# Scores ahead of attention, smaller pieces of weight work among VectorE's steps, and products of ones on TensorE in a fused attention and expert kernel

## The reference, cut to what matters

```python
# attention, ctx the 64 context rows of a sequence
kp = ctx @ Wk.T; vp = ctx @ Wv.T + bv; qp = layernorm(x) @ Wq.T + bq
x = x + softmax(qp @ kp.T / sqrt(128)) @ vp @ Wo.T + bo
# experts, E = 8, K = 2, F = 512
t = layernorm(x)
probs, idx = top_k(softmax(t @ Wr + br), 2); probs = probs / probs.sum()
h = layernorm(relu(t @ W1[e] + b1[e])) * g1[e] + be1[e]
y = layernorm(relu(h @ W2[e] + b2[e])) * g2[e] + be2[e]
x = x + sum over the 2 experts of probs * y
```

## Time and profile before

| | us |
|---|---|
| timed runs, median (lowest to highest) | 297.57 (297.2 to 300.11) |
| profiled execution | 300.53 |
| its span, first to last instruction | 298.8 |
| TensorE busy | 247.1 |
| VectorE busy | 246.1 |
| ScalarE busy | 215.3 |
| GpSimd busy | 192.2 |

### The profile page before, as it was taken

How to read it: one execution, slowest core, us unless ns; L and a number is a source line. 1 busy time by engine, 2 the same in 40 slices (tenths; PEclk the granted TensorE clock), 3 DMA queues, 4 the chain that set the end, 5 groups by cost and what they waited for, 6 DMA issues and landing times.

```text
span 298.8 us, 9992 instructions
## 1 busy us (share of the span) xinstructions
PE 247.1 (83%) x2765; PEld 193.0 (65%) x2768; DVE 246.1 (82%) x1109; ACT 215.3 (72%) x799; POOL 192.2 (64%) x302
## 2 busy tenths in 40 slices
PE   2788558898799767976987999999999797999980
PEld 2354346555466534456876988999999786999520
DVE  0758947765678698987998989999999797999996
ACT  1355536674945768864989998999999797999820
POOL 8802275746463655777676876788887675878550
PEclk9999655557855775699999999999999999999995
DMA  6996294121311332345222323233334656452338
GB/s 171 340 289 206 63 313 154 55 64 54 125 53 53 91 107 71 88 95 127 57 65 53 77 62 74 57 76 75 75 73 66 185 146 134 130 145 65 98 114 281
DMA packets 48801, 34.56 MB, mean 116 GB/s; under 512 B 26934, under 2 KB 42870, under 8 KB 48747
## 3 DMA queue, kind: packets, MB, share of 16 engines
q1 hardware_dynamic: 39100, 22.83, 27.7%
q0 software_dynamic: 6592, 9.00, 10.7%
q10 hardware_dynamic: 3056, 2.11, 2.4%
HBM read 15.14 MB, written 12.02 MB: 91 GB/s over the span
## 4 chain that ended last, share of the span: by engine, by line
PE 31%; POOL 22%; issue 16%; DVE 11%; DMA 7%; SPq 6%; ACT 5%; POOLq 2%; DVEq 0%; ACTq 0%
PE bank L726 13%; PE bank L730 13%; POOL answers L684 10%; POOL words_of L710 7%; POOL slot_rows L672 4%; SPq L520 4%; PE bank L791 2%; DMA x_tok<-in_x 2%; DMA kb_room<-slot_rows 2%; SPq L553 1%; DVE w2f L1620 1%; DMA answers<-vo,words_of 1%; PE bank L776 1%; DMA w_mean<-w_sums 1%; ACT w1l L1193 1%
## 5 line engine op out<-in xcount | busy, mean ns | idle before, releaser
L672 POOL DMA_INDIRECT slot_rows<-pay,pos x64 | 65.8, 1027 | 44.8 <-DVE pos L1575 27.4
L684 POOL DMA_INDIRECT answers<-vo,words_of x71 | 69.8, 984 | 32.4 <-ACT vo L1363 21.2
L726 PE MATMUL bank<-kb_room,w1h 128*128 128x128 f16 x568 | 55.0, 219 | 9.2 <-DMA kb_room<-slot_rows 3.8
L730 PE MATMUL bank<-w2h,rh 128*128 x284 | 51.4, 219 | 2.2 <-ACT w2l L1099 1.6
L726 PEld LDWEIGHTS bank<-kb_room,w1h 128*128 x568 | 42.2, 97 | 15.9 <-issue 10.4
L730 PE MATMUL bank<-rh 128*128 128x129 f16 x284 | 51.5, 220 | 0.0
L730 PE MATMUL bank<-w2l,rh 128*128 x284 | 51.4, 219 | 0.0
L726 PE MATMUL bank<-kb_room,w1l 128*128 128x128 f16 x284 | 51.1, 219 | 0.0
L1321 ACT ACTIVATE rh<-bank 128x512 f16<-128x512 f32 x71 | 41.9, 590 | 11.3 <-PE bank L726 9.5
L1839 DVE SCALAR_TENSOR_TENSOR xk<-bank,rh 128x512 f16<-128x512 f32 x71 | 47.9, 674 | 0.0
L710 POOL DMA_DIRECT2D words_of<-slot_rows x71 | 40.7, 575 | 4.9 <-issue 4.6
(11 more groups left out here) (260 smaller groups left out, 612.3 us busy)
## 6 DMA issues: line engine op xcount, KB each, us to landing
x_tok<-in_x SPq DMA_DIRECT2D x8, 256.0 KB, 6.8
w1f<-in_L_ffn_W SPq DMA_DIRECT2D x2, 1024.0 KB, 9.3
pay<-pay SPq DMA_DIRECT2D x8, 256.0 KB, 2.7
w1f<-answers SPq DMA_DIRECT2D x8, 256.0 KB
w2f<-answers SPq DMA_DIRECT2D x8, 256.0 KB, 3.3
kb_room<-slot_rows SPq DMA_TRANSPOSE x71
words_of<-slot_rows POOLq DMA_DIRECT2D x71, 1.0 KB
answers<-vo,words_of POOLq DMA_INDIRECT x71
```

The costliest lines, as they stand in the source:

```text
L672: eng.indirect_dma_start(slot_words, bass.IndirectOffsetOnAxis(ap=pos[:, g % 2, k, i:i + 1], axis=0), pay[g % 2][:, k, i, :].bitcast(U32), ...
L684: eng.indirect_dma_start(answers, bass.IndirectOffsetOnAxis(ap=words_of[:, j % NW, 0:1], axis=0), z[j % NZ], None).then_inc(s_ans[j % NZ], 16)
L726: return eng.matmul(dst, lhsT, rhs, start=start, stop=stop)
L730: return eng.matmul(dst, lhsT, rhs, start=start, stop=False, skip_group_check=True)
```

## The change

- The scores of a group become one bias product of 256 columns and four products of 64 columns into bank 1, with keys in a tile of their own (`kq`). The 136 columns of x and its logits become a product of their own (`skip`) into banks 3 and 4. From step 2 on, two of the next group's four scores stand ahead of `attend`, two behind it; `skip` comes at the step's end. The maxima are one reduction over 256 columns instead of two over 128, and stand ahead of the statistics.
- `base_next` moves to the head of a step, `totals` with it in step 5.
- `keep(n)` is new: n bf16 products of ones, 128 by 128, into columns of bank 2 that nothing reads: 12 ahead of the first ranks, 10 ahead of the probabilities' transpose in steps 1 to 7, and 10 ahead of the ranks in steps 3 to 8.
- VectorE's tables name 22 places in a step and single pieces: `CENTRE` numbers the 32 pieces of W2. Its pieces now stand in steps 5 to 7. `weight_scale` is taken apart among the root steps of step 5; the gate's steps are taken apart around `picked` and `pos_`.
- SP makes the payload's copy ahead of the transfers of W2's sums, and the second of these in step 5 of its loop instead of 6; ScalarE's `w_rows_copy(0)` moves behind `x2_copy` in step 4.
- The tiles that lay in parts of `xk` (`part_rows`, `parts`, `shares` and others) get room of their own, and GpSimd's copy of identities into `xk` goes.

```diff
@@ -444,10 +440,16 @@
-        NONE = ((),) * 4
...
-        CENTRE = {4: ((), (), (), (0,)), 5: ((), (1,), (2,), (3,)), 6: ((), (), (4,), (5,)), 7: ((6,), (), (7,), ())}
...
+        LESS_LAST = {2: {2: (0,), 16: (1,), 17: (2,), 21: (3,)}, 3: {3: (4,), 5: (5,), 7: (6,), 9: (7,)}}
...
+        UP_LO = {7: {14: (3,)}, 8: {4: (4,), 6: (5,), 8: (6,), 10: (7,)}}
...
@@ -729,6 +727,13 @@
                 return eng.matmul(dst, lhsT, rhs, start=start, stop=False, skip_group_check=True)
+            ones_b = ones[:, :].bitcast(BF16)[:, 0:P]
+            def keep(n):
+                for _ in range(n):
+                    mm(bank[2][:, 3 * P:], ones_b, ones_b)
             done = []
             def ctxT(h):
...
@@ -776,25 +781,32 @@
                     t = eng.transpose(bank[0][:, i * P:(i + 1) * P], x[:, g * GT + i, :], ident[:, :])
                 t.then_inc(p_xT, 1)
-            def scores(g, b):
+            def score_bias(g):
                 n, first = (0, 0) if g * GT < FIRST else (1, FIRST)
-                if 2 * g + b >= 3:
-                    eng.wait_ge(s_x2, 2 * g + b - 2)
-                if g in (0, FIRST // GT) and b == 0:
+                if g >= 1:
+                    eng.wait_ge(s_prob, g)
+                if g in (0, FIRST // GT):
                     eng.wait_ge(s_sel, n + 1)
                     from_act(eng, f"sdT{n}")
-                    eng.wait_ge(s_ones, 4)
-                tiles = range(2 * b, 2 * b + 2)
-                at = g * GT + 2 * b - first
-                eng.matmul(pair(g, b)[:, :, 0:KEYS], sdT[n][:, :], kb_tile[n][:, at:at + 2, :], start=True, stop=False,
-                           skip_group_check=True)
+                mm(bank[1][:, 0:GT * KEYS], sdT[n][:, :],
+                   kb_tile[n][:, g * GT - first:(g + 1) * GT - first, :].rearrange("p i k -> p (i k)"), stop=False)
+            def score_of(g, tiles):
                 eng.wait_ge(s_xT, g + 1)
                 for i in tiles:
-                    t = mm_beside(pair(g, b)[:, i % 2, :], xT[g % 2][:, i * P:(i + 1) * P], xk[:, 2 * g + b, :])
-                if b == 1:
+                    b = 2 * g + i // 2
+                    t = mm(bank[1][:, i * KEYS:(i + 1) * KEYS], xT[g % 2][:, i * P:(i + 1) * P],
+                           kq[:, b * KEYS:(b + 1) * KEYS], False, i == GT - 1)
+                if GT - 1 in tiles:
                     t.then_inc(p_score, 1)
+            def skip(g):
+                if g >= 1:
+                    eng.wait_ge(s_x2, g)
+                for i in range(GT):
+                    mm_beside(attn(i // 2, i % 2), xT[g % 2][:, i * P:(i + 1) * P], ident_wr[:, :], i % 2 == 0)
             def probT(g):
                 eng.wait_ge(s_norm, g + 1)
...
@@ -927,26 +939,37 @@
             ends(p_setup, PE_SETUP, "wvo", done,
                  mm(bank[7][0:1, 256:256 + D + E], bcol[:, 2:3], ident_wr[:, :], start=False))
             from_act(eng, "keys0")
-            scores(0, 0)
-            scores(0, 1)
+            score_bias(0)
+            score_of(0, range(GT))
             values(0)
+            skip(0)
             xT_(1)
             probT(0)
             from_act(eng, "values0")
             attend(0)
-            scores(1, 0)
-            scores(1, 1)
+            score_bias(1)
+            score_of(1, range(GT))
             key_bias(1)
             keys(1)
             gains()
             base_start()
             xT_(2)
+            skip(1)
             for n in range(1, GROUPS + 1):
                 if n == 1:
+                    keep(12)
                     ranks(0)
+                if n >= 2:
+                    base_next(n - 2)
+                if n == 5:
+                    totals()
                 if n < GROUPS:
+                    keep(10)
                     probT(n)
+                    if 1 < n < GROUPS - 1:
+                        score_bias(n + 1)
+                        score_of(n + 1, range(GT // 2))
                     if n in (3, 6):
                         from_act(eng, f"values{n // 3}")
                     attend(n)
...
@@ -954,27 +977,27 @@
                     sd_rows(1)
                     from_act(eng, "keys1")
                 if n == 2:
-                    base_next(0)
                     ranks(1)
+                if n == 1:
+                    score_bias(n + 1)
                 if n < GROUPS - 1:
-                    scores(n + 1, 0)
+                    score_of(n + 1, range(GT // 2 if n > 1 else 0, GT))
                 if n > 2:
-                    base_next(n - 2)
                     if n == GROUPS:
                         down_low(0)
                         down_low(1)
+                    keep(10)
                     ranks(n - 1)
                 if n < GROUPS - 2:
                     xT_(n + 2)
                 if n < GROUPS - 1:
-                    scores(n + 1, 1)
+                    skip(n + 1)
                 if n == 2:
                     values(1)
                 if n == 3:
                     w_rows(0, 0)
                     w_rows(0, 1)
                 if n == 4:
-                    totals()
                     w_rows(1, 0)
                 if n == 5:
                     w_rows(1, 1)
...
@@ -1491,15 +1522,22 @@
                 eng.wait_ge(q_sum, sums.n)
                 eng.tensor_tensor(prob[:, :, :], ex[:, :, :], per_key(rsum[:, :]), ALU.mult).then_inc(s_norm, 1)
-            def stats2(g):
-                eng.wait_ge(s_x2, 2 * g + 2)
+            def stats2(g, scores=None):
+                if scores is not None:
+                    maxima(scores)
+                eng.wait_ge(s_x2, g + 1)
                 for i in range(GT):
                     t = eng.bn_stats(st[:, i, :], x2[:, g * GT + i, 0:D])
+                    if i == 0 and scores is not None:
+                        max_scaled(scores)
                 stat.up(t)
+                weights(g + 1, 0)
                 eng.wait_ge(q_stat, stat.n)
                 for i in range(GT):
                     t = eng.bn_aggr(mv[:, i, :], st[:, i, :])
                 stat.up(t)
+                weights(g + 1, 1)
                 eng.wait_ge(q_stat, stat.n)
                 if g >= 1:
                     eng.wait_ge(s_guess2, g)
...
@@ -1781,31 +1833,35 @@
             eng.wait_ge(s_const, 1)
             for n in range(1, GROUPS + 1):
-                if 2 < n < GROUPS:
-                    max_(n)
-                stats2(n - 1)
-                weights(n, 0)
+                stats2(n - 1, n if 2 < n < GROUPS else None)
+                weights(n, 2)
                 if 2 < n < GROUPS:
                     normed(n)
-                if n == 5:
-                    weight_scale()
                 if n <= 2:
                     max_(n)
                 for k in range(7):
                     root2_(k, n - 1)
+                    if n == 5:
+                        weight_scale(k)
                     if n == GROUPS - 2:
                         whole_places(k)
+                    weights(n, 3 + k)
                 logits(n - 1)
+                weights(n, 10)
                 logits_bias(n - 1)
+                weights(n, 11)
                 if n == 2:
                     normed(2)
                 top_max(n - 1)
+                weights(n, 12)
                 gate_diff(n - 1)
-                weights(n, 1)
                 top_index(n - 1)
+                weights(n, 13)
                 top_hot(n - 1)
+                weights(n, 14)
                 if n == AHEAD + 1:
                     whole_tiles()
+                weights(n, 15)
                 top_mask(n - 1)
                 if n == 1:
                     normed(1)
```

176 lines of the change are left out of this document (98 added, 78 removed).

## The result

The changed kernel took 281.99 us, median of four runs (279.82 to 285.83), beside 297.97 for the kernel before (four runs; the first three have the median 297.57); the ratio is 0.943, 95% interval 0.934 to 0.951. This ratio and all that follow leave out executions that lie more than 1.5% above the fastest of their kernel. A second series on another chip gave 0.948 (0.931 to 0.964). I had predicted 288.1 (a ratio of 0.968) and a range from 283 to 296: the direction was right, the gain is 16 us instead of 9.5, and the median lies a microsecond under the range. The profiled execution is the longest of the four, at 285.83 us; one of the second series took 280.36, and its starts are given beside the first's where they matter.

The account below looks back on a forecast made before the run. A chain through the groups before the slots, with no engine full, was taken to bound the kernel. Terms -12.8 + 2.1 - 1.0 + 2.2 = -9.5 us gave 288.1 us against the median; range 283 to 296.

Parts of the forecast that it names:

- Scores ahead: Before the slots: splitting off 64 score columns ahead of the other 136 removes 7.2 us of VectorE's waits before the maxima.
- G(2): Start of group 2's first exponential on ScalarE: forecast 38 for 42.27.
- G(3): Start of group 3's first exponential on ScalarE, after W2's landing and its squares: forecast 48.0, 6.3 us earlier.
- G(3) to G(5): Time from group 3's first exponential to group 5's: forecast 25.0 us for 25.5.
- G(5): Start of group 5's first exponential on ScalarE, 79.79 before: forecast 6.8 us earlier.
- my lower bound of 23.4: Groups 3 to 5, first exponential to first exponential: 23.4 us if TensorE's clock is up before W2's column sums.
- partial hold: Products of ones hold TensorE's clock up only partly: 2.2 us of delay to ranks and positions.
- G(5) to the last guess: From group 5's first exponential to the last group's root guess: forecast 34.3 us for 40.3, gain 6.0.
- Last step: Last group, root guess to first slot's ReLU: four low halves of W1 between root steps, +2.1 and -1.0 us.
- the clock held throughout: Rival: TensorE's clock stays near 1.0 to the end of the groups, 284.3 us; chance 0.17.
- the slower rival: Products of ones burden a full TensorE whose clock from 36 to 120 stays put: about +3.5, 301.1 us; chance 0.12.
- Slots, SP, GpSimd: Slots keep their 169.5 us; SP's copies and fetches are reordered; GpSimd, with 27.4 us of waits, does not bind.

Follow-up runs that it names:

- late signal: The changed kernel with VectorE's maxima released by the 136-column products instead of the 64-column scores: 293.98 us, 0.993 of the kernel before.
- scores alone: The changed kernel without its products of ones and with the pieces of W2 and W1 in runs of four; moved sums and copies stay: 284.14 us.

## Why the prediction was too small

*Scores ahead, G(2) and G(3).* Right: 37.6 and 47.8 (35.5 and 45.7 in the second profile), forecast 38 and 48.0. The 7.2 us of waits went; most of the gain at G(2) is step 1, 10.5 us for 14.5. There the late signal shows what the maxima's wait was worth, 3.6 us; for the later steps no run shows it. Next late ahead of G(3) was W2's landing: ScalarE waited 1.5 us for it, as forecast.

*G(3) to G(5).* This step failed: 25.0 us forecast, 21.97 measured, below even my lower bound of 23.4. Two things were wrong in it: how step 3 adds up on VectorE, and the path through TensorE's column sums. I added step 3 up along ScalarE and put all four subtractions between the root steps at full length on top of the root steps: 3.8 us. Measured:

```profile
50.16 0.16 DVE L1467 TENSOR_TENSOR yy<-y 128x4 f32<-128x4 f32 x1
...
52.77 0.16 DVE L1556 SCALAR_TENSOR_TENSOR nmr<-mv,rstd 128x4 f32<-128x4 f32 x1
```

2.8 us from the first root step to the end of the last. Only three subtractions lie between them, and each adds 0.48 us instead of 0.63, since two dependent steps start 0.20 apart in any case and 0.68 with a subtraction between them. That made step 3 11.2 us instead of 12.3.

Secondly, G(5) does not come from that sum at all. TensorE reached the column sums 9.4 us after G(3), they took 4.6, and G(5) followed 7.95 later: 22.0. Before, these three were 11.2, 6.9 and 7.3: 25.5. What the shorter root steps gave is in the first of them, for the ranks ahead of the sums wait for VectorE's mask (1.9 us at 55.6), which stands behind the root steps. I had named this path, but took a value between the clock's two levels, and even my case at the higher level, 23.4, had too little off the way to the sums. In both profiles of the change on the chips without pauses the sums ran wholly at the higher level. Where they ran at the lower one, in the kernel with scores behind attention, G(3) to G(5) was 25.8 us, close to my 25.0; with ones alone in the old order, at the higher one again, it was 21.2. The level is not certain for the change either: in its profile on the second chip with pauses the sums took 1.86 + 4.97 us.

*The clock.* I took 2.2 us off the gain for a partial hold, and made the hold depend on the ones. No such delay appears, and the ones are only part of the hold: the clock was 0.60 before, 0.70 with the scores alone, 0.75 without ones and 0.84 with them, and from 0.75 to 0.84 the time did not follow. What the ones do cost is 0.5 us in step 4, where I had rightly said that the transposes stand behind them. Why the new order raises the clock by itself no run shows.

*G(5) to the last guess.* 33.0 us (31.3 in the second profile) for a forecast of 34.3: the term was 1.3 too large. I had filled it with 33 us of VectorE, from its 31.9 before and four more pieces; it is busy 27.8 in it, so VectorE is not what fills these steps. Two reasons can be read: the stretch before held one low half of W1 and part of a group's statistics more, and a piece between two dependent steps adds 0.14 us (0.34 from start to start instead of 0.20), not its 0.29. I had left the second without a figure. The 9.2 us that I counted into the 31.9 are all 32 pieces; the 28 in that stretch were 8.0.

*Last step.* Forecast +2.1 - 1.0 = +1.1; measured 10.3 instead of 9.3, and 9.2 in every kernel that has the old place of these pieces. Right.

*The sum.* Forecast 119.9 for the ReLU, measured 113.14. The difference of 6.8 is 3.2 up to G(5), 1.3 from there to the guess and 2.2 of clock. The slots were 1.4 us longer in that execution. The nearest of my rivals was the clock held throughout, 284.3; it too was too high, and its condition, a clock near 1.0, was not met at 0.84. The condition of the slower rival, a mean clock not above 0.6, did not come about, and the ones mostly fall into waits for VectorE: even twice as many made only two steps longer.

*Slots, SP, GpSimd.* Right: the slots kept their length within 1.4 us (within 0.2 in the second profile), and GpSimd still waits.

## What to carry over

Sum a step up along each engine that can end it, to the same event, and take the latest: here G(5) was TensorE's, while I had added along ScalarE. If an engine has two speeds, its long blocks are worth pricing at each, for a reordering may itself move it to the faster one, as it did here for a reason that stays open. Work put in only to fill pauses should be priced in the new order: the ones that gave 2% to the old order gave nothing to the new. And before an experiment puts one signal back, look at what now stands ahead of it in every step, the first one too: here the setup's products did, and made up the larger part of the loss.

## What I had not expected of the hardware

On two chips the kernel before took 337 us, 13% more, and the change 17 to 18% more. In the profiles of the changed kernels there (the kernel before was not profiled) much of it lay in pauses ahead of instructions whose inputs were long ready. In the changed kernel's step 4 there, TensorE had finished the transposed probabilities at 72.3, and ScalarE had been idle since 70.8:

```profile
71.92 0.39 PE L816 MATMUL bank<-ident_wr,prob 128*128 128x128 f32 x2
```

```profile
79.35 0.38 ACT L1122 ACTIVATE pT<-bank 128x256 f32<-128x256 f32 x1 [8.59 <-remote]
```

Five such waits of that one copy made 27.9 us from 36 to 120; in the profiles of the change and of the kernel before on the other chips there is none. The profile names no instruction of this core as the releaser, and I could not find the cause. A kernel whose steps are paced by such a pause would gain little from a shorter chain, which fits the change's 1 to 2% there; that is argued, not shown. A comparison of variants that few per cent separate has to be made on one chip, and the kernel before's own time has to be looked at first.
